# The first columns of a banded attention kernel: one pair in the first chunk, later column loads behind the first rows

## The reference, cut to what matters

```
scores = einsum("bhcqd,bhckd->bhcqk", qc, kc)      # qc, kc, vc: blocks of 32 tokens, 96 keys around them
valid = (abs(rel) <= w) & (k_pos >= 0) & (k_pos < S)
p = softmax(where(valid, scores, -1e9), axis=-1)
out = einsum("bhcqk,bhckd->bhcqd", p, vc)
x1 = layernorm(x + out) * g1 + b1
x2 = layernorm(x1 + relu(x1 @ W1 + b1) @ W2 + b2) * g2 + b2
x3 = layernorm(x + x2)
out = layernorm(x3 + product_key_ffn(x3))          # 8 heads, 8 of 32 x 32 keys, experts of 128 numbers
```

## Time and profile before

| what | value |
|---|---|
| median of 3 runs | 651.7 us (648.76 to 651.85) |
| the profiled execution | 650.28 us |
| its span in the trace | 648.5 us |
| PE busy | 520.1 us (80%) |
| DVE busy | 541.3 us (83%) |
| ACT busy | 410.9 us (63%) |
| POOL busy | 402.2 us (62%) |

### The profile page before, as it was taken

How to read it: one execution, slowest core, us unless ns; L and a number is a source line. 1 busy time by engine, 2 the same in 40 slices (tenths; PEclk the granted TensorE clock), 3 DMA queues, 4 the chain that set the end, 5 groups by cost and what they waited for, 6 DMA issues and landing times.

```text
span 648.5 us, 42547 instructions
## 1 busy us (share of the span) xinstructions
PE 520.1 (80%) x17953; PEld 443.2 (68%) x17985; DVE 541.3 (83%) x1741; ACT 410.9 (63%) x813; POOL 402.2 (62%) x522
## 2 busy tenths in 40 slices
PE   0279999999998899994567888887787788778776
PEld 0158878888886577784346777776776777667676
DVE  5658989889897577864788889999999999999992
ACT  4246766677775557764164576677677668667764
POOL 8345546555552235442267768878878887887882
PEclk9989999999998999996667799999999999999999
DMA  6877975654516001000012223322332332233231
GB/s 201 246 221 233 285 206 172 188 191 148 195 56 226 17 18 33 17 1 5 5 45 54 66 48 81 77 61 64 77 76 49 81 77 58 68 77 76 50 77 44
DMA packets 45201, 64.39 MB, mean 99 GB/s; under 512 B 5488, under 2 KB 37360, under 8 KB 42608
## 3 DMA queue, kind: packets, MB, share of 16 engines
q1 hardware_dynamic: 45168, 63.97, 35.7%
HBM read 36.29 MB, written 8.65 MB: 69 GB/s over the span
## 4 chain that ended last, share of the span: by engine, by line
PE 40%; issue 17%; ACT 17%; POOL 12%; DVE 9%; DMA 3%; POOLq 1%; ACTq 1%; SPq 0%; another core or an unknown queue 0%; DVEq 0%
PE ps L754 8%; PE ps L813 5%; ACT early L1070 5%; PE ps L734 4%; ACT tile_rows L1082 4%; PE ps L769 4%; PE ps L826 4%; PE ps L744 3%; ACT L1070 3%; POOL tile_rows L663 3%; PE ps L919 3%; POOL rstd L690 2%; PE ps L780 2%; DMA xT<-terms 2%; PE ps L928 2%
## 5 line engine op out<-in xcount | busy, mean ns | idle before, releaser
L919 PE MATMUL ps<-arena,hid 128*32 128x32 f32 x8192 | 79.6, 200 | 53.8 <-DVE hid L1437 46.8
L919 PEld LDWEIGHTS ps<-arena,hid 128*32 128x32 f32 x8192 | 75.7, 112 | 60.0 <-issue 31.1
L968 ACT ACTIVATE arena<-ps 128x512 f32<-128x512 f32 x128 | 69.8, 595 | 54.3 <-PE ps L754 54.1
L928 PEld LDWEIGHTS ps<-xT,downT_sb 128*128 128x128 f32 x528 | 69.0, 204 | 13.5 <-issue 12.4
L1178 DVE TENSOR_REDUCE row_max<-ps 128x8 f32<-128x768 f32 x64 | 61.0, 953 | 17.5 <-PE ps L744 17.2
L928 PE MATMUL ps<-xT,downT_sb 128*128 (+1 forms) x528 | 68.7, 287 | 1.8 <-issue 0.2
L754 PE MATMUL ps<-ident,arena 128*128 128x128 f32 x512 | 69.3, 280 | 0.0
L940 PE MATMUL ps<-up_sb,prod 128*128 128x128 f32 x512 | 65.6, 282 | 0.3 <-DVE prod L1446 0.3
L1181 DVE TENSOR_TENSOR arena<-ps,row_max 128x768 f32<-128x768 f32 x64 | 61.3, 958 | 5.1 <-DVE row_max L1178 0.2
L669 POOL TENSOR_TENSOR wq_sb<-wq_sb,tile_rows 128x1024 f32<-128x1024 f32 x32 | 64.6, 2018 | 1.0 <-POOL tile_rows L663 0.4
L940 PEld LDWEIGHTS ps<-up_sb,prod 128*128 128x128 f32 x512 | 62.9, 196 | 0.5 <-DVE prod L1446 0.5
(11 more groups left out here) (161 smaller groups left out, 1332.5 us busy)
## 6 DMA issues: line engine op xcount, KB each, us to landing
arena<-r_x SPq DMA_DIRECT2D x128, 128.0 KB, 2.4
early<-terms SPq DMA_DIRECT2D x8, 720.0 KB
xT<-terms SPq DMA_DIRECT2D x8, 720.0 KB
hid<-terms SPq DMA_DIRECT2D x8, 720.0 KB
prod<-terms SPq DMA_DIRECT2D x8, 720.0 KB
x_pair<-in_x_wrapped SPq DMA_DIRECT2D x16, 256.0 KB, 4.5
xT_tile<-xT SPq DMA_DIRECT2D x34, 64.0 KB, 1.9
x<-in_x SPq DMA_DIRECT2D x8, 256.0 KB, 2.9
```

Source lines behind the costliest of these rows:

```text
L919: mm = nc.tensor.matmul(slots[32 * g:32 * g + 32, k, c], leftT[p][:, r // 2, r % 2, :], blocks_of[p][:, :, r // 2, r % 2, GROUP * g:GROUP ...
L928: mm = nc.tensor.matmul(ps[:, 4 + half, (c % 4) * P:(c % 4 + 1) * P], downT_sb[:, c * P:(c + 1) * P], xT[:, tok(t)].rearrange("p (q r k) - ...
L968: return nc.scalar.activation(out_ap, in_ap, ACT.Copy)
```

## The change

Chunk 0 now holds one pair instead of two, chunk 1 three instead of two; the sum of columns is nearly the same. At the start SP issues only the column loads of chunks 0 and 1. That of chunk 2 follows the term writes of pair 0, and those of chunks 3 and 4 follow the rows of pair 0 and its values. The rows of pair 0 wait for two cleared buffers, not four, and for the writes of one pair. The term writes of chunk 1 move ahead of the rows of pair 1, which now wait for them (pair 1 is in chunk 1), and for all four cleared buffers. ACT and DVE split chunks 0 to 3 before attention; the four steps of chunk 4 are put into the first pair of attention, high and rest after tile 0's turn, middle and low after tile 1's. The constant `row_heads` is made after the splits.

```diff
-    CHUNKS = ((0, 2), (2, 4), (4, 8), (8, 12), (12, 16))
+    CHUNKS = ((0, 1), (1, 4), (4, 8), (8, 12), (12, 16))
...
-            for c in range(5):
+            def x_columns_in(c):
                 sp.dma_start(x_f32[c], xT_wrapped[:, COLS[c]]).then_inc(x_f32_in[c], 16)
+
+            for c in range(2):
+                x_columns_in(c)
...
                 if i == 0:
                     keep_terms(0)
-                    sp.wait_ge(rows_cleared, 4)
-                    sp.wait_ge(terms_out[0], 64)
+                    x_columns_in(2)
+                    sp.wait_ge(rows_cleared, 2)
+                    sp.wait_ge(terms_out[0], 32)
                     rows(0)
                     x_load(0, 0)
+                    for c in (3, 4):
+                        x_columns_in(c)
+                    keep_terms(1)
+                    sp.wait_ge(rows_cleared, 4)
+                    sp.wait_ge(terms_out[1], 96)
                     rows(1)
                     x_load(1, 1)
-                    keep_terms(1)
                     continue
...
-            for c in range(5):
+            def high_terms(c):
                 a.wait_ge(x_f32_in[c], 16)
                 copy(x_terms[c][:, 0], x_f32[c]).then_inc(x_high, 1)
+
+            def mid_terms(c):
                 a.wait_ge(x_rest, c + 1)
                 copy(x_terms[c][:, 1], x_f32[c]).then_inc(x_mid, 1)
+
+            for c in range(4):
+                high_terms(c)
+                mid_terms(c)
...
                     if not (last and p == 1):
                         exps(2 * i + p + 1, 1 - p)
+                    if first:
+                        (high_terms, mid_terms)[p](4)
...
-            V.tensor_copy(row_heads[:], stretch(fold4[:, 0:1], P))
...
-            for c in range(1, 5):
+            for c in range(1, 4):
                 split_x(c)
+            V.tensor_copy(row_heads[:], stretch(fold4[:, 0:1], P))
             shift(0, 0, 0)
...
                     normalise(t, p, 1)
+                    if first:
+                        (rest_terms, low_terms)[p](4)
```

More of the change, by code:

```diff
@@ L1150, in _, with rest_terms, low_terms, split_x @@
             v.wait_ge(consts_ready, 3)
-            V.tensor_copy(row_heads[:], stretch(fold4[:, 0:1], P))
             v.sem_inc(r1_done, 2)
             v.sem_inc(norm_done, 2)
-            def split_x(c):
+            def rest_terms(c):
                 v.wait_ge(x_high, c + 1)
                 V.tensor_tensor(x_f32[c], x_f32[c], x_terms[c][:, 0], ALU.subtract).then_inc(x_rest, 1)
+            def low_terms(c):
                 v.wait_ge(x_mid, c + 1)
                 V.tensor_tensor(x_terms[c][:, 2], x_f32[c], x_terms[c][:, 1], ALU.subtract).then_inc(x_split, 1)
+            def split_x(c):
+                rest_terms(c)
+                low_terms(c)
             split_x(0)
```

## The result

| what | before | after |
|---|---|---|
| median, 22 runs each | 650.48 us (648.76 to 654.35) | 654.56 us (649.45 to 662.45) |
| ratio, 95% interval | | 1.0053 [1.0035, 1.0072] |
| the profiled execution, its span | 650.28, 648.5 us | 656.31, 654.5 us |
| DVE's maximum of tile 0 / 2 / 12 / 31 begins | 28.32 / 41.24 / 98.22 / 199.00 | 27.57 / 45.32 / 102.12 / 202.89 |

The run of 662.45 us was in a slower state of the chip and is left out of the ratio; the median of the other 21 is 654.26 us. The kernel is 3.4 us slower (0.0053 x 650.5). The last line of the table says where, in the two profiled executions: tile 0 is 0.75 us earlier, tile 2 is 4.1 us later, and this lateness is carried nearly unchanged (3.9 us) to the last tile.

The account below looks back on a forecast made before the run. The prediction took POOL's memsets and SP's term writes to bound the start, then pair 1's late rows to decide: +2.6 us on the profiled 650.28 gives 652.9, stated as 653.0 us for the median, range 647.5 to 657.5.

Parts of the forecast that it names:

- my likeliest class: Whole kernel: time within 0.5% of the kernel before, chance 0.54; slower had 0.34, faster 0.12.
- What bounds the start: Start: POOL's four memsets and SP's term writes end within 0.3 us; only a change moving both gains.
- Pair 0: Start: pair 0's rows issued at 9.8 instead of 13.66, 3.9 us earlier, in POOL's hands at 20.5.
- Pair 0 does not get through DVE sooner: First tile: chunk 3's columns arrive at 23.2, its split takes 5.1 us, first maximum 28.6 against 28.32 before.
- Pair 1's rows: Rows wait for chunk 1's writes, landing at 29.1 (lower end 24.8); at POOL 39.8, tile 2 at 43.8, 2.6 us later.
- PE's 2.78 us without instructions: PE's stop inside tile 2: taken as hidden in the over 4 us wait for tile 2; otherwise added on top.
- Chunk 4 inside attention: Chunk 4's split in DVE's and ACT's free time: 0 us; without that cover 1.3 to 2.6 us.
- The waits for tiles 6 and 12: POOL's later waits for rows move with the tiles: 0, up to 1 us either way.
- The blocked queue: Rival: SP's queue stalls issuing chunk 1's six writes, 4.7 us later than forecast, 657.6, centre 656; chance 0.34.
- The kept head start: Rival: chunk 1's writes land at 24.8, tile 2 comes 1.7 us earlier, at best 646.4 us; chance 0.15.

Follow-up runs that it names:

- Experiment 7: Kernel before with only row_heads made after the splits; ratio 0.9969 to the kernel before.
- Experiments 3: Kernel before with row_heads made after the splits and pair 0's rows waiting for two cleared buffers, not four; ratio 0.9989 to the kernel before.
- Experiment 2: Changed kernel with all five column loads at the start again; ratio 1.0027 to the kernel before.
- experiment 1: Changed kernel with POOL's copy of tile 1's edge values moved ahead of tile 2's row copies; ratio 0.9978 to the kernel before.
- experiment 8: Changed kernel with chunk 4 split ahead of the first tile again; ratio 1.0048 to the kernel before.
- experiment 4: As 9, plus column loads moved: chunk 2 at the start, chunk 3 ahead of pair 0's rows, chunk 4 behind pair 1's; ratio 0.9997 to the kernel before.
- 9: Changed kernel with tile 1's edge values ahead on POOL and only pair 1's term writes ahead of its rows; ratio 1.0031 to the kernel before.
- experiment 6: Changed kernel with only pair 1's two term writes ahead of its rows, those of pairs 2 and 3 behind; ratio 1.0023 to the kernel before.
- 5: Kernel before with tile 1's edge values copied ahead of tile 2's rows on POOL; ratio 1.0009 to the kernel before.
- 10: Kernel before with row_heads late, pair 0's rows waiting for two cleared buffers, and tile 1's edge values ahead on POOL; ratio 0.9960 to the kernel before.
- 1b: The kernel of experiment 1 timed again on another chip; ratio 1.0012 to the kernel before.
- experiment 12: As experiment 4, but with chunk 1's six term writes kept together as in the changed kernel; ratio 0.9975 to the kernel before.

## Why the prediction was right in size, in part by luck, and wrong in one step

I gave 653.0 us and 647.5 to 657.5; it was 654.56. The shift forecast was 2.6 us, the ratio gives 3.4. The ratio, 1.0053, lies at the border between my likeliest class (within 0.5%) and slower.

- **What bounds the start: half right.** I wrote that only a change that moves both POOL's memsets and SP's writes gains anything. Experiment 7 moved the writes alone, and pair 0 was there 1.3 us sooner in its one profiled execution, though its rows left no earlier.
- **Pair 0: right.** Rows issued at 9.54 (9.8 said), in POOL's hands at 20.38 (20.5). The subtraction wasn't held: it took 0.49 us. Experiments 3 and 7 show that `row_heads` had held it, since with 576 columns it took 0.76 us. By the Trainium skill, page "SBUF — State Buffer", section "SBUF: two separate sides", the cast is held by the memset and the subtraction isn't. The traces agree in this: the cast took 2.22 us beside the memset and 0.31 at its new place, the subtraction 0.49 beside it. They don't agree on the whole of it: held until the memset's end at 7.05, the cast would have put the end of the old subtraction near 7.8, and it was 7.13.
- **Pair 0 does not get through DVE sooner: right.** First maximum at 27.57 (28.6 said, 28.32 before). Chunk 3's columns arrived at 21.9 (23.2), and its split took 5.5 us (5.1). Experiment 2 shows the link.
- **Pair 1's rows: right in kind, said 2.6 us too late.** The writes had landed at 27.0, between my lower end of 24.8 (whose 1.5 us for the acknowledgement is in no row) and the 29.1 that I chose. My reason for calling 29.1 the right way of pricing, that twelve engines hold the rows' backlog alone, is neither shown nor refuted by this, as no view shows single engines. Then came 10.15 us to POOL (10.7). So pair 1 was there at 37.16, not 39.8. Had only this counted, tile 2 would have come at 37.16 + 4.0 = 41.2, no later than before, which is what experiment 1 shows (40.55 and 40.93). The missed mechanism cost 4.1 us, and the 2.6 us by which I put the rows too late made up for most of it; that tile 2 came within 1.5 us of my 43.8 is luck.
- **The failed step: "PE's 2.78 us without instructions ... I take them as hidden now, as PE stands at the wait for tile 2 for over 4 us."** PE stood earlier, at tile 0's values, since the block of values that they need is made by POOL behind the copies that wait for pair 1. I had priced POOL's wait only by what it waits for and not by what is queued behind it. The gap wasn't hidden either: 1.59 us of it stayed. What the runs showed in its place: tile 2's scores 4.9 us late, less 0.9 us on the way to DVE (1.2 of it the shorter gap), is 4.1 us where I had 2.6.
- **Chunk 4 inside attention: right**, 0 as far as experiment 8 can tell. **The waits for tiles 6 and 12: right**; tile 12's moved with the tiles, 6.17 us for 5.93, and 56.8 us lie between tiles 2 and 12 as against 57.0 before.
- **The rivals.** The blocked queue did not happen: SP took 8.43 us for the six writes and was done at 21.4, before they had landed. The kept head start did not either, but experiment 4 built most of it: even with tile 2 at 37.25, it was gone by tile 12.

## What to carry to other kernels

When a change makes a transfer late, list what stands in program order behind the instruction that will wait for it, on its engine, and ask for each who needs it; here a copy of 0.29 us with its input long present cost more than the late rows themselves. A head start at the front of a pipeline is worth only what the slowest stream behind it lets through (argued here from the waits in experiments 4 and 9): look at the next waits for the same kind of transfer before counting it. Where a change has several parts, time the smallest by itself; here one moved line measured 0.31% less than before, and the whole 0.53% more.

## What the hardware showed that I had not expected

- **PE's gap without instructions ends 4 to 6.5 us after the start of tile 0's values.** It was 5.1 us in the kernel before, 4.5 in the kernel after, and 6.4, 5.8, 5.8, 5.8, 5.4, 5.3, 4.7, 4.4 and 4.2 in experiments 6, 3, 4, 7, 5, 10, 2, 8 and 9, while the gap's end itself lies anywhere from 36.4 to 44.5. Between these two points the transfers of before, after and experiment 6 hold one instruction packet each. In experiment 6, from 37.9 to 44.3 us (packets, MB, share of 16 engines):

```profile
q1 hardware_dynamic: 432, 1.30, 68.8%
q8 instruction: 1, 0.02, 0.9%
```

  That PE asks for the next block of its program only when it takes up the values would fit these, and the gap at tile 2 was gone in experiments 1, 1b and 12, where PE waited 1.6 us or more for rows at that point; experiment 12 has a stop of 2.37 us inside tile 0's values instead. But it is not shown: such a packet also stands in stretches in which PE doesn't stop (30 to 35.3 us in the kernel before), and what starts the transfer was not tried by itself.
- **A subtraction of DVE and a copy of POOL lengthen each other as if one waited for the other to end.** In the kernel after, the 128x1088 subtraction began at 23.09 beside a POOL copy that ended at 23.8, and took 1.86 us instead of 1.29; it ended at 24.95, 1.2 us behind that copy. POOL's next copy took 2.52 instead of 1.47, to 26.27, 1.3 us behind the subtraction. In experiment 1 it was 2.46 us from 38.16, beside a copy up to 39.5, and then 2.10 instead of 1.04. The Trainium skill, page "SBUF — State Buffer", section "SBUF: two separate sides", calls this an exclusive lock for an instruction of DVE with two inputs in SBUF against one of POOL that reads SBUF; the traces agree within 0.2 us.
- **Issuing behind transfers that are still under way takes SP long**, 8.43, 13.23 and 16.27 us for six to eight writes, where four took 2.22 us at the start. In the kernel after and in experiment 12, POOL's waits up to 75 us name no transfer that SP issued behind these writes.
- **PE came out of the stall at half clock.** The view of stretches for the kernel after (columns as in the earlier trace rows):

```profile
40.00:42.00 2.00, 2.00 (x154) 2.00 (x157) 0.43 (x2) 0.00 (x0) 2.00 (x2) 0.50 0.94 310
42.00:45.00 3.00, 1.41 (x54) 1.00 (x49) 1.63 (x3) 0.00 (x0) 0.74 (x3) 0.50 0.92 271
```

  Granted is 0.50, the level of 1.2 GHz, after 4.36 us without work; it was 1.00 from 33 to 35.6 us. In experiment 6 it was 0.50 after a wait of 2.87 us, in experiment 1 still 1.00 after one of 2.98, so the length of the wait alone doesn't decide it. The values of tile 0 took 2.15 us here and 1.85 before, at 1.00, and the 27 matmuls of tile 2 took 0.75 us and 0.49. How much of the 4.1 us at tile 2 this makes isn't shown, since the gap behind these matmuls takes up part of it.
